# Mamba and MoE stage on one core: six of a group's 32 products of the scanned state with C made on GpSimd instead of VectorE

## The reference

```python
dA = jnp.exp(delta[..., None] * A)
dBx = delta[..., None] * Bm[:, :, None, :] * xc[..., None]
def step(h, inp):
    dA_t, dBx_t, c_t = inp
    h = dA_t * h + dBx_t
    y = jnp.einsum('bdn,bn->bd', h, c_t)
    return (h, y)
```

## Time and profile before

| | us |
|---|---|
| median of 3 runs (lowest, highest) | 2898.72 (2897.68, 2898.99) |
| the profiled execution | 2897.52 |
| its span, first to last instruction | 2895.8 |
| PE busy (matmul records) | 2564.7 |
| PE weight loads busy | 1279.0 |
| VectorE busy | 2097.2 |
| ScalarE busy | 1476.2 |
| GpSimd busy | 1730.1 |

### The profile page before, as it was taken

The page is one execution under the profiler, slowest core; times in us unless marked ns, Lnnn a source line. Parts: engine busy times, 40 slices in busy tenths (PEclk is TensorE's granted clock), DMA queues, the critical chain, the costliest instruction groups (busy, mean ns, idle before and its releaser), DMA issues. The chain is left out here.

```text
span 2895.8 us, 29805 instructions
## 1 busy us (share of the span) xinstructions
PE 2564.7 (89%) x7998; PEld 1279.0 (44%) x7999; DVE 2097.2 (72%) x2271; ACT 1476.2 (51%) x2733; POOL 1730.1 (60%) x864
## 2 busy tenths in 40 slices
PE   4589898988989989889898898976499999999999
PEld 2134343343433434334343343432266666666665
DVE  0399999999999999999999999999322222222222
ACT  1566766667666676666766667664122222222222
POOL 1467787787887878878778787786222222222222
PEclk9799999999999999999999999999699999999999
DMA  1303314133141331413304133031522222222221
GB/s 40 133 34 112 122 38 145 57 118 128 32 145 63 112 129 31 146 63 112 134 28 145 69 105 136 23 138 58 195 46 43 44 44 44 44 45 43 45 45 29
DMA packets 125604, 236.15 MB, mean 82 GB/s; under 512 B 46449, under 2 KB 93714, under 8 KB 109122
## 3 DMA queue, kind: packets, MB, share of 16 engines
q1 hardware_dynamic: 98342, 200.56, 20.2%
q0 software_dynamic: 26128, 34.36, 6.9%
q10 hardware_dynamic: 1036, 0.09, 0.0%
HBM read 182.22 MB, written 53.78 MB: 81 GB/s over the span
## 5 line engine op out<-in xcount | busy, mean ns | idle before, releaser
L515 POOL TENSOR_TENSOR arena<-u,arena 128x2048 f32<-128x2048 f32 x256 | 1160.0, 4531 | 351.8 <-DVE psum L914 348.6
L914 DVE TENSOR_TENSOR_SCAN psum<-psum,arena 128x1024 f32<-128x1024 f32 x512 | 1171.3, 2288 | 62.3 <-ACT psum L707 34.4
L1295 PE MATMUL psum<-hc,ident 128*128 128x512 f32 x2048 | 1003.9, 613 | 238.1 <-DVE hc L922 237.7
L1295 PEld LDWEIGHTS psum<-hc,ident 128*128 128x128 f32 x2048 | 356.5, 191 | 751.9 <-DVE hc L922 468.6
L707 ACT ACTIVATE psum<-delta,a_neg 128x508 f32<-128x508 f32 x1024 | 656.5, 674 | 0.6
L922 DVE TENSOR_TENSOR hc<-psum,arena 128x1024 f32<-128x1024 f32 x512 | 624.8, 1220 | 9.9
L590 POOL DMA_INDIRECT out_dram<-hres,tok_id x136 | 211.8, 1557 | 598.7 <-ACT hres L849 545.2
L1429 PE MATMUL psum<-arena,xnt 128*128 x1088 | 515.6, 596 | 0.0
L1181 DVE COPY z<-psum 128x512 f32<-128x512 f32 x136 | 94.1, 692 | 458.1 <-PE psum L1438 458.1
L849 ACT ACTIVATE hres<-psum,tok_w 128x256 f32<-128x256 f32 x136 | 64.5, 474 | 454.4 <-PE psum L1448 447.7
L1448 PE MATMUL psum<-arena,z 128*128 x1088 | 257.1, 379 | 0.9 <-DVE z L1181 0.9
(11 more groups left out here) (144 smaller groups left out, 1952.2 us busy)
## 6 DMA issues: line engine op xcount, KB each, us to landing
arena<-ssm_rows SPq DMA_DIRECT2D x128, 1024.0 KB, 5.8
delta<-expert_rows SPq DMA_DIRECT2D x136, 129.0 KB, 2.1
h_saved_rows<-hnew SPq DMA_DIRECT2D x16, 512.0 KB, 6.7
hres<-h_saved_rows SPq DMA_DIRECT2D x16, 512.0 KB, 3.5
out_dram<-h SPq DMA_DIRECT2D x16, 512.0 KB
draw<-ssm_rows SPq DMA_DIRECT2D x16, 256.0 KB, 3.3
arena<-in_L_ffn_wg_dram SPq DMA_DIRECT2D x8, 512.0 KB
arena<-in_L_ffn_wi_dram SPq DMA_DIRECT2D x8, 512.0 KB
```

The costliest lines, as they stand in the source:

```text
L515: pool.tensor_tensor(dBx[k % 2], rep, b_rep[:, q * QN:(q + 1) * QN, :], ALU.mult).then_inc(dbx_ready, 1)
L914: nc.vector.tensor_tensor_scan(h, h, src, 0.0, ALU.mult, ALU.add).then_inc(scan_done, 1)
L1295: last = nc.tensor.matmul(yacc[(k // HC) % 2], ident[:, :], hc[k % 2][:, i, :], start=False, stop=(k % HC == HC - 1 and i == 1))
```

## The change

For half units 13, 16, 18, 21, 22 and 25 the scan writes its result into an SBUF buffer instead of back into PSUM, and GpSimd multiplies it there by the C rows, in place. The buffers are `hnew` (13, 18), `hres` (16), `xn` (21, 25) and `h2` (22). VectorE waits before such a scan until the buffer is free (`state_free`). PE adds these six later, behind the sums of half units 17, 19, 20, 24, 25 and 29 (`DONE_WITH`). ScalarE's exponential k may start once scan k-2 is done where k-2 is one of the six. `hc` alternates over the other 26. GpSimd's own steps are moved: delta and u of chunks 1 to 3 from behind units 1, 4, 8 to behind units 3, 6, 11; the scatters from units 2, 3, 5, 6 to 1, 2, 4, 5; the six products stand behind units 8, 9, 10, 12, 13, 14. SyncE's first C load of the next group waits for product 25 as well, and the loads of `hres`, ScalarE's evacuations and the first norm get waits for the sums that free their buffers.

```diff
+        ON_POOL = {13: hnew, 16: hres, 18: hnew, 21: xn, 22: h2, 25: xn}
+        DONE_WITH = {17: 13, 19: 16, 20: 18, 24: 21, 25: 22, 29: 25}
...
             def load_hres(g, saves):
                 sp.wait_ge(emb_full, 2 * saves)
+                sp.wait_ge(sum_done, HU * g + nth_sum[16] + 1)
...
-                    ahead(sp, hc_ready, HU * (g - 1) + HU - HC + 2 * q + 2)
+                    for k in (HU - HC + 2 * q, HU - HC + 2 * q + 1):
+                        if k in ON_POOL:
+                            ahead(sp, hc_pool, NPL * (g - 1) + nth_pool[k] + 1)
+                        else:
+                            ahead(sp, hc_ready, NOWN * (g - 1) + nth_own[k] + 1)
...
+            def times_c(g, k):
+                pool.wait_ge(scan_done, HU * g + k + 1)
+                j = k % HC
+                if k < HC:
+                    pool.wait_ge(c_loaded[j // 2], 16 * (g + 1))
+                state = ON_POOL[k][:, :, :].rearrange("p b c -> p (b c)")
+                pool.tensor_tensor(state, state, flat(c_rep[:, 2 * j:2 * j + 2, :]), ALU.mult).then_inc(hc_pool, 1)
...
-                    if k in (1, 4, 8):
-                        c = {1: 1, 4: 2, 8: 3}[k]
+                    if k in (3, 6, 11):
+                        c = {3: 1, 6: 2, 11: 3}[k]
...
+                    if k in (8, 9, 10, 12, 13, 14):
+                        times_c(g, {8: 13, 9: 16, 10: 18, 12: 21, 13: 22, 14: 25}[k])
...
-                ahead(actq, hc_ready, HU * g + k - 1)
+                if k >= 2 and k - 2 in ON_POOL:
+                    actq.wait_ge(scan_done, HU * g + k - 1)
+                elif k >= 2:
+                    actq.wait_ge(hc_ready, NOWN * g + nth_own[k - 2] + 1)
...
-                nc.vector.tensor_tensor_scan(h, h, src, 0.0, ALU.mult, ALU.add).then_inc(scan_done, 1)
+                if k in ON_POOL:
+                    state_free(g, k)
+                    out_ = ON_POOL[k][:, :, :].rearrange("p b c -> p (b c)")
+                else:
+                    out_ = h
+                nc.vector.tensor_tensor_scan(out_, h, src, 0.0, ALU.mult, ALU.add).then_inc(scan_done, 1)
+
+            def state_free(g, k):
+                if k == 13:
+                    dve.wait_ge(xn_ready, min(g + 2, G))
+                    dve.wait_ge(h_saved, 16 * min(g + 2, G))
...
+                if k == 21:
+                    dve.wait_ge(xnt_full, NK * min(g + 2, G))
+                    ahead(dve, l_full, g)
+                if k == 22:
+                    ahead(dve, row_ready, g)
+                    ahead(dve, h2_stored, 16 * g)
...
-                    add_state(g, k)
+                    if k not in ON_POOL:
+                        add_state(g, k)
+                    if k in DONE_WITH:
+                        add_state(g, DONE_WITH[k])
```

More of the change, by code:

```diff
@@ L169, in audio_tower @@
         emb_pair = [bank_a, bank_b]
+        ON_POOL = {13: hnew, 16: hres, 18: hnew, 21: xn, 22: h2, 25: xn}
+        DONE_WITH = {17: 13, 19: 16, 20: 18, 24: 21, 25: 22, 29: 25}
+        OWN = [k for k in range(HU) if k not in ON_POOL]
+        NOWN, NPL = len(OWN), len(ON_POOL)
+        nth_own = {k: i for i, k in enumerate(OWN)}
+        nth_pool = {k: i for i, k in enumerate(ON_POOL)}
+        SUMS = [k for at in range(HU) for k in (at, DONE_WITH.get(at)) if k in nth_own and k == at or k != at and k in ON_POOL]
+        nth_sum = {k: i for i, k in enumerate(SUMS)}
+        LAST_SUM = [max(nth_sum[k] for k in range(HC * c, HC * c + HC)) for c in range(NCH)]
+        assert len(SUMS) == HU and NOWN % 2 == 0 and not ON_POOL.keys() & {0, 1, HU - 2, HU - 1}
         def scratch(i):
@@ L628, in norm1 @@
                     ahead(actq, xnt_full, NK * g)
+                    ahead(actq, sum_done, HU * (g - 2) + nth_sum[25] + 1)
                     ahead(actq, l_full, g - 2)
@@ L916, in times_c @@
             def times_c(g, k):
-                j = k % HC
+                if k in ON_POOL:
+                    return
+                j, n = k % HC, nth_own[k]
                 dve.wait_ge(scan_done, HU * g + k + 1)
-                if k < HC and k % 2 == 0:
+                if k < HC and (k % 2 == 0 or k - 1 in ON_POOL):
                     dve.wait_ge(c_loaded[k // 2], 16 * (g + 1))
-                ahead(dve, sum_done, HU * g + k - 1)
-                nc.vector.tensor_tensor(flat(hc[k % 2][:, :, :]), flat(dA[k % 2]), flat(c_rep[:, 2 * j:2 * j + 2, :]),
+                if n >= 2:
+                    dve.wait_ge(sum_done, HU * g + nth_sum[OWN[n - 2]] + 1)
+                else:
+                    ahead(dve, sum_done, HU * (g - 1) + nth_sum[OWN[NOWN + n - 2]] + 1)
@@ L1292, in add_state @@
             def add_state(g, k):
-                pe.wait_ge(hc_ready, HU * g + k + 1)
+                if k in ON_POOL:
+                    pe.wait_ge(hc_pool, NPL * g + nth_pool[k] + 1)
+                    state = ON_POOL[k][:, :, :].rearrange("p (i b) c -> p i (b c)", i=2)
+                else:
+                    pe.wait_ge(hc_ready, NOWN * g + nth_own[k] + 1)
+                    state = hc[nth_own[k] % 2]
+                c = k // HC
                 for i in range(2):
-                    last = nc.tensor.matmul(yacc[(k // HC) % 2], ident[:, :], hc[k % 2][:, i, :], start=False,
-                                            stop=(k % HC == HC - 1 and i == 1))
+                    last = nc.tensor.matmul(yacc[c % 2], ident[:, :], state[:, i, :], start=False,
+                                            stop=(nth_sum[k] == LAST_SUM[c] and i == 1))
                 last.then_inc(sum_done, 1)
```

34 lines of the change are left out of this document (25 added, 9 removed).

## The result

| | before | after |
|---|---|---|
| median of 4 runs (lowest, highest), us | 2898.20 (2895.63, 2898.99) | 2945.54 (2944.02, 2946.22) |
| the profiled execution, its span | 2897.52, 2895.8 | 2946.22, 2944.2 |
| VectorE busy | 2097.2 | 1988.6 |
| GpSimd busy | 1730.1 | 1949.6 |
| last gate of the first stage | 2036.2 | 2083.3 |

The ratio is 1.0166, with a 95% interval of 1.0151 to 1.0182: 47 us slower, where 52 us faster was forecast. The whole difference is in the first stage, which ends 47.1 us later. VectorE was relieved of 108.6 us of work and the program still got longer.

What follows compares the result with a forecast made beforehand. VectorE was taken to set the pace, with PE and ScalarE equally loaded between half units 12 and 21. 14 x 3.1 + 2 x 4.5 = 52 us off 2898.7 gave 2846 us, range 2795 to 2872.

Steps and rivals of the forecast that it cites:

- SyncE: Loads and new waits for free buffers: later C rows and buffer events at least two half units back cost nothing.
- PE* step: PE's matmuls followed from product 12: the convolution of half unit 18 starts 0.64 us earlier, at 1025.75.
- The walk: The prediction's step-by-step timing of one middle group through PE, ScalarE, GpSimd and VectorE: 3.1 us gained, group 117.0 us.
- GpSimd's places: GpSimd's order of dBx and products: dBx 13 ends at 1049.6, scan 26 wants it at 1050, so it holds.
- The chain to scan 21: PE's convolution through ScalarE to exponential 21 is unbroken, so scan 21 moves 0.65 us earlier, to 1036.0.
- the products of 18 and 25 give nothing: Scan 27 waits about 1.4 us, losing product 25's 1.26; products 13, 16 and 18 leave only 0.65 at scan 21.
- The wait of 1 to 1.5 us before scan 27: Expected sign on VectorE: a new wait of this size, since add 21 delays the second embedding and exponential 27.
- 2 x 4.5 us: First and last group: GpSimd's dBx 13 for scan 26 limits the gain to 4.5 us each.
- VectorE alone: Rival: VectorE sets the pace, exponentials 21 and 27 aren't late, 7.56 to 8.45 us a group, 2764 to 2778; 10%.
- Nothing is left: Rival: PE or GpSimd slips further, scan 21 doesn't move, time stays at 2893 to 2903 us; 3%.
- GpSimd blocked by scans into SBUF: Rival: GpSimd stands still during the six scans writing SBUF, group 125.4 us, time 2984; 7%, with other ways to be slower.

## Why the prediction was wrong, point by point

**The step that failed** is the sentence in *SyncE*: "The new waits for free buffers (hnew, hres, xn, h2) name events that lie at least two half units back; nothing." The distance in half units of the data was counted, not what PE has to do before it: sum 13 stands behind sum 17, which needs product 17, the last thing VectorE does before scan 18. The *PE* step had the times in hand ("add 17 ... 24.0, add 13 25.75"). It would have put scan 18 at 1025.8, where VectorE could have started it at about 1022.3. The walk never sent that number back to VectorE. What followed from it, "PE reaches x_ssm ... at 1033.9, its old place", failed with it: x_ssm starts 35.3 us behind scan 12 in place of 31.5, and scan 23 stands 40.8 us behind it in place of 38.1.

**A second term was missing:** the clock. It stood at 1.00 in the rows read the earlier trace rows, and the walk took 1.72 us for every sum. Relieved of products, PE got new gaps, and sums at half clock.

The 5.9 us between the group predicted (117.05) and found (122.93) come apart as follows.

| | us of a group | from |
|---|---|---|
| error of the walk without either | 0.5 | 117.54 in groups with no lowered clock, two kernels with four products |
| scan 25 waits for sum 21 | 2.4 | 119.93 - 117.54 |
| scan 18 waits for sum 13 | 1.3 | what is left |
| half clock at sum 19 | 1.7 | 123.18 - 121.50, in the change with filling matmuls |

The last two are the least certain. The drop cost 1.1 us in the kernel with only sum 13 early; by that the wait for sum 13 is 1.9. A group with no lowered clock takes 121.50 us with both waits (and the filling matmuls) and 119.93 with the later one alone, 1.6 us apart. The sum of the two rows, 3.0, is firm (122.93 - 119.93). The walk's own 0.5 us lies behind scan 23, which stands 38.10 us behind scan 12 in the groups of 117.54 us, where the walk put it (38.1). Times 16 groups the whole is 94 us; the forecast missed by 99.5, and the four earliest of the 13 middle groups, with up to 10 us at half clock and 123.1 to 123.7 us, are part of the rest.

**What held.** GpSimd's product takes 2.34 to 2.39 us (taken: 2.36) and GpSimd is busy for 108.0 us of a group (108). Scans into SBUF take 2.26 to 2.29.

```profile
L559 POOL TENSOR_TENSOR xn<-xn,arena x32: 2337/2352/2367, 204.7 to 2063.7; 128x1024 f32<-128x1024 f32 x32
L559 POOL TENSOR_TENSOR hres<-hres,arena x16: 2347/2371/2385, 182.2 to 2025.8; 128x1024 f32<-128x1024 f32 x16
```

GpSimd's places hold: no scan of a middle group waits for dBx, also with both waits gone. The evacuation of xi is exposed for 0.69 us (walked: 0.85). The chain to scan 21 is confirmed: with early sums scan 21 stands 33.39 us behind scan 12, with six products and with four (walked: 33.6, before: 34.25). That the products of 18 and 25 give nothing is too: the shortest groups take 117.54 us with six products and with four. The SyncE loads of C are not waited for. The wait of 1 to 1.5 us before scan 27 exists, as 0.77 or 0.99 before 26 and 0.27 before 27. For the first and the last group the forecast had 2 x 4.5 us. With four products and the gap filled the last gate of the first stage comes 47.2 us earlier (1989.0 in place of 2036.2); less 14 x 2.6 that leaves 10.8 us.

**The rivals.** *VectorE alone* fell: with both waits and the clock out of the way VectorE is busy for 112.81 of 117.54 us, and the group doesn't shrink below that. The groups with no lowered clock gain 2.6 us each, where that rival wants 7.56 and more for six products (5.04 for the four that were measured so), and the waits for ScalarE behind PE's queue remain. The Trainium skill, Perfetto Trace Analysis, Identifying the Most-Contended Engine, says to optimize the engine with the highest occupancy first, here VectorE; the trace doesn't bear it out, since 108.6 us less on VectorE came with 47 us more in all. *Nothing is left* came near in time for one kernel (only 21 and 22), but by the clock and not by GpSimd. *GpSimd blocked by scans into SBUF* named the right sign and the wrong place: dBx takes 4.527 us in the mean, before 4.531, so nothing blocks it. The Trainium skill, SBUF — State Buffer, Who interferes with whom, says that a VectorE instruction with at most one SBUF input, outside the two-port modes, doesn't contend with GpSimd; the trace agrees. The 7% given to a slower kernel was argued from GpSimd alone; a loss of this size through PE's queue is in none of the rivals.

**Open.** Why the clock falls at just these places isn't settled. What the rows show is what PE did before: few short matmuls, and gaps of 0.8 to 3.3 us, but the gap ahead of sum 19 could be closed without effect, and kernels alike but for an early sum drop in different places. Nor does a gap suffice: the kernel before idles up to 1.58 us on PE within a middle group, and the kernel with only sum 13 early has groups with no lowered clock and this gap ahead of sum 26:

```profile
1065.11 1.98 PE L1369 MATMUL psum<-hc,ident 128*128 128x512 f32 x4 [3.27 <-DVE hc L990]
```

What in the history of a group tips it is not known. No run here has six products, early sums and filling matmuls only around half unit 19, so whether six products can reach the 2852 us of four is open.

## What to carry to other kernels

A wait for a reused buffer costs what stands ahead of its reader in the reader's queue, counted from the newest input that queue needs, and not from the age of the data: write the release time into the walk of the engine that waits. Here two sums placed one half unit earlier, behind work that is already possible, turned 47 us of loss into 28 us of gain. And where an edit moves or opens gaps on TensorE, read the granted clock of the stretch afterwards. Filling matmuls are to be tried and measured one place at a time: of four kernels with them here, one gained 21 us and three lost 6 to 19.

## What the runs showed of the hardware that was not expected

- Half clock (0.50) came for 3.4 us or 6.8 us at a time in middle groups of 11 of the 13 kernels other than the one before, behind gaps and short matmuls on PE; in the change PE is busy for 89% of a group by its matmul records. In the kernel before, none of 13 middle groups has it. A drop of 3.4 us cost 0.8 (118.37 - 117.55), 1.1 or 1.7 us of a group where PE was in the chain, and nothing in the 117.55 us groups of the kernel with early sums, where it falls around half units 27 and 28.
- A gap of 3.27 us on PE ahead of sum 26 has the full clock (1.00) in the groups of 119.93 us of the kernel with only sum 13 early.
- Two zero-weight matmuls, 1.72 us, in the gap of 2.06 us ended the drops in all 13 middle groups: 2873 to 2852 us. The same ahead of half units 19 and 26, or 28, did not.
- A scan of 1,024 columns takes 2.26 to 2.30 us into PSUM and 2.26 to 2.29 into SBUF. dBx on GpSimd takes 4.50 to 4.57 us with such scans beside it, as before (4.51 to 4.57).
